# Contextual attention on one core: the additions of the shifted copies move from VectorE to GpSimd

## The reference

```
f = b[:, :, ::2, ::2]                       # 40 x 40
w = 3x3 patches of f                        # L = 1600 patches of 64*9
wn = w / max(|w|, 1e-4)
yi = einsum(w, wn) * mm                     # 1600 x 1600 scores
yi = softmax(10 * yi over the patches) * mm
patches = einsum(yi, 4x4 patches of b with stride 2)
out = the patches added up where they overlap (stride 2), cropped, / 4
```

## Time and profile before

| | |
|---|---|
| median of 3 runs | 1432.39 us |
| the profiled execution | 1435.39 us, its span 1433.6 us |
| TensorE busy | 1327.2 us (93%) |
| VectorE busy | 1183.3 us (83%) |
| ScalarE busy | 857.9 us (60%) |
| GpSimd busy | 46.9 us (3%) |
| line 979 on VectorE | 448 additions, 247.6 us |
| line 1109 on GpSimd | 56 copies, 42.9 us |

### The profile page before, as it was taken

The page is one execution under the profiler, slowest core; times in us unless marked ns, Lnnn a source line. Parts: engine busy times, 40 slices in busy tenths (PEclk is TensorE's granted clock), DMA queues, the critical chain, the costliest instruction groups (busy, mean ns, idle before and its releaser), DMA issues.

```text
span 1433.6 us, 24384 instructions
## 1 busy us (share of the span) xinstructions
PE 1327.2 (93%) x7190; PEld 894.6 (62%) x7190; DVE 1183.3 (83%) x2827; ACT 857.9 (60%) x2233; POOL 46.9 (3%) x62
## 2 busy tenths in 40 slices
PE   4988999999999899999999899999999999998886
PEld 4756765676556665577656676567655766566433
DVE  3667889799888898889897888979987898978983
ACT  2677646676557565586565764666655855658331
POOL 1000000010000100001000000001000010000100
PEclk9997999999999999999999999999999999999998
DMA  5502482145822556135741359224572236313442
GB/s 91 89 1 85 109 173 76 47 116 119 163 64 67 124 113 150 49 86 127 143 117 33 104 118 179 70 52 110 126 156 67 71 107 135 94 32 96 131 136 53
DMA packets 180471, 142.54 MB, mean 99 GB/s; under 512 B 119859, under 2 KB 177267, under 8 KB 180339
## 3 DMA queue, kind: packets, MB, share of 16 engines
q1 hardware_dynamic: 180178, 140.50, 41.7%
q10 hardware_dynamic: 160, 0.49, 0.2%
HBM read 19.76 MB, written 13.11 MB: 23 GB/s over the span
## 4 chain that ended last, share of the span: by engine, by line
PE 54%; DVE 15%; ACT 11%; issue 8%; SPq 7%; DMA 5%; DVEq 0%; POOL 0%; ACTq 0%; POOLq 0%
PE psO L521 26%; PE psG L471 23%; SPq L326 4%; DVE G L968 4%; ACT S L697 4%; DVE Z L1001 3%; DMA SH<-G 3%; PE psG L480 3%; DVE S L898 3%; ACT G L708 2%; ACT G L683 2%; DVE G L979 2%; DMA SHJ<-G 2%; SPq L270 1%; ACT SQ L624 1%
## 5 line engine op out<-in xcount | busy, mean ns | idle before, releaser
L521 PE MATMUL psO<-Z,B 123*128 123x492 f32 (+2 forms) x1792 | 718.6, 530 | 46.0 <-DVE Z L1001 31.4
L521 PEld LDWEIGHTS psO<-Z,B 123*128 123x128 f32 x1792 | 325.8, 194 | 247.6 <-issue 133.8
L471 PE MATMUL psG<-LH,HL 128*123 128x246 f16 (+2 forms) x2616 | 407.2, 285 | 3.7 <-ACT G L670 3.0
L697 ACT ACTIVATE S<-S,nm 123x480 f32<-123x480 f32 (+3 forms) x560 | 308.5, 555 | 161.2 <-DVE nm L905 160.8
L471 PEld LDWEIGHTS psG<-LH,HL 128*123 128x123 f16 x2616 | 277.4, 137 | 125.4 <-issue 64.5
L708 ACT ACTIVATE G<-G,nb 123x492 f32<-123x492 f32 (+1 forms) x448 | 265.0, 639 | 60.3 <-DVE G L968 59.9
L898 DVE CUSTOM_DVE_ANT_0 S<-G,RB 123x492 f32<-123x492 f32 (+1 forms) x448 | 268.4, 604 | 25.8 <-ACT G L683 15.6
L979 DVE TENSOR_TENSOR G<-G,SH 123x492 f32<-123x492 f32 (+1 forms) x448 | 247.6, 591 | 48.9 <-DMA SH<-G 48.3
L968 DVE SCALAR_TENSOR_TENSOR G<-G,RA,psB 123x492 f32<-123x492 f32 (+1 forms) x448 | 270.4, 647 | 0.0
L883 DVE TENSOR_TENSOR G<-G,psG 123x492 f32<-123x492 f32 (+2 forms) x272 | 135.0, 496 | 90.4 <-PE psG L471 46.5
L1001 DVE TENSOR_TENSOR Z<-G 123x984 f32<-123x984 f32 (+2 forms) x192 | 197.2, 1028 | 0.0
(11 more groups left out here) (79 smaller groups left out, 575.8 us busy)
## 6 DMA issues: line engine op xcount, KB each, us to landing
SH<-G SPq DMA_DIRECT2D x336, 214.8 KB
SH<-G SPq DMA_DIRECT2D x112, 89.2 KB
SH<-G SPq DMA_DIRECT2D x336, 19.2 KB
XP<-x SPq DMA_DIRECT2D x20, 280.0 KB, 5.7
XP<-mid SPq DMA_DIRECT2D x20, 280.0 KB, 5.5
HL<-LH SPq DMA_DIRECT2D x16, 246.5 KB, 4.5
mid<-OSB SPq DMA_DIRECT2D x48, 80.0 KB, 2.3
out<-OSB SPq DMA_DIRECT2D x48, 80.0 KB, 2.3
```

What stands on the lines that cost most here:

```text
L471: last = pe.matmul(psG[0:TW, bank, b0 * TW:b1 * TW], st[:, v % 2, p:p + TW], mv[:, v % 2, lo:lo + n], start=i == 0, stop=i == len(terms) - 1)
L521: last = pe.matmul(psO[:, b, 0:n], B[:, o:o + 128], Z[:, 2 * (s % 2) + j, 0:n], start=t == 0, stop=t == TILES - 1)
L697: last = act.activation(y, y, ACT.Exp, bias=nm[:, k * TILES + t:k * TILES + t + 1], accum_out=sg[:, c:c + 1])
```

## The change

GpSimd makes the additions of line 979 in place of VectorE. They stand first in GpSimd's slots, ahead of the wraps, and are those of pair s + 3 in slot s (AHEAD was 2). Order, tiles, operands, waits and counts of each addition are as before; no other engine's order is changed. The wraps stay in their slots.

```diff
-AHEAD = 2
+AHEAD = 3
...
-            def add_shifted(at):        # in VectorE's block
...
-                    at_y = place(u, v, s + AHEAD)
-                    if at_y:
-                        add_shifted(at_y)
                     at_z = place(u, v, s + 1)
                     if at_z:
                         sum_pair(at_z, s + 1)
...
+            def add_shifted(at):        # in GpSimd's block
+                u, k, i = at
+                c0, n = p_cols(k)
+                for j, t in enumerate(arg_tiles(i)):
+                    o = k * TILES + 2 * i + j
+                    pool.wait_ge(sh_in[o % SFREE], (u * (NB // SFREE) + o // SFREE + 1) * 16 * len(SHIFT_PARTS))
+                    g = G[:, t * GLEN + c0:t * GLEN + c0 + n]
+                    pool.tensor_tensor(g, g, SH[:, o % SFREE, 0:n], ALU.add).then_inc(y1_made, 1)
+
             def body(u, v):
                 for s in BODY:
+                    at = place(u, v, s + AHEAD)
+                    if at:
+                        add_shifted(at)
                     if s < 5 and u is not None:
                         wrap(u, s + 2)
```

More of the change, by code:

```diff
@@ L970, in argument_pair @@
                                              op0=ALU.mult, op1=ALU.subtract).then_inc(arg_made, 1)
-            def add_shifted(at):
[L973 to L979, removed]
             def sum_pair(at, s):
```

## The result

The change made the kernel slower. Eight runs after have a median of 1438.85 us (1436.86 to 1443.50), eight runs before 1430.06 us (1426.80 to 1433.05); the ratio is 1.0066, with a 95% interval of 1.0048 to 1.0085. The forecast was 1419 us, faster. The profiled execution after took 1443.5 us, the longest of its eight; the one before, 1435.39 us, is likewise longer than its eight.

What follows compares the result with a forecast made beforehand. TensorE and VectorE were taken as both full mid-image, with winnable time where TensorE waits for VectorE's Z. Borders 8, clock 3, last image 2, middles 0 us: -13 us, 1419 us for the median, own range 1409 to 1428 (chance 0.48).

Steps and rivals of the forecast that it cites:

- (4) Middles: 0: Middle of an image: TensorE is full and hides VectorE's relief, so the change gains 0 us there.
- 7 us, hidden: A pair's four DMAs (2.9 us), landing (2.0) and two additions (2.2) fit in the 12 us before the first sum.
- a gain for SP: SP's 236.8 us of waits for line 979 to free SH slots would shrink, as GpSimd frees them once data lands.
- Speed of GpSimd: A GpSimd addition of 492 columns takes 1.1 us, between 0.73 and 1.46, fast enough for slots of 6.1 us.
- Price of the lock, in the mean: VectorE's operations with two SBUF inputs (lines 898, 1001) wait for GpSimd's reads: 0.6 us a slot, between 0 and 2.2.
- Relief of VectorE: VectorE loses a pair's additions, 1.16 us a slot; net of the lock's price 0.56 us a slot.
- Term 1: Eight borders between images, where VectorE is full and TensorE waits for Z: 1.0 us gained at each, 8 us.
- the first rival: Nothing gained: GpSimd's additions fall on the border's last two of line 898; 1432 us, chance 0.16.
- Term 2: Around the borders, shorter TensorE idle time keeps its clock up at some: a quarter of 12 us, 3 us.
- Term 3: Last image, only shifts, sums and pastes, TensorE and VectorE both full: 2 us gained.
- A larger AHEAD only says where the additions stand before the wraps: GpSimd's own order: AHEAD of 3 has no cost, since GpSimd has no pace but its waits.
- The third: Slower if lock waits pass 1.16 us a slot, at lines 898 and 1001 around borders: 1444 us, chance 0.18.

Runs made afterwards that it cites:

- pieces and AHEAD = 3: Changed kernel with the loads as one DMA in each of slots 2 to 4 and 9 to 14: 1428.41 us, 0.9976 of the kernel before.
- small loads: Loads from the second unit on bring one row: changed kernel 1418.82 us, kernel before with the same loads 1425.30 us; ratio of the two 0.9966.
- memset_long: Changed kernel with each GpSimd addition replaced by writing zeros of about the same time, additions left out: 1406.74 us, 0.9823 of the kernel before.

## Why the prediction was wrong

The direction was wrong: 9 us slower, where 13 us faster was forecast. Of the 22 us between them, about 14 come with the traffic of the loads, a term that the sum did not have, and 8 are gains that were put too high.

**The step that failed** is "(4) Middles: 0", with the chain "7 us, hidden" and the mean price of the lock that it rests on. The chain of four issues, a landing and two additions was worked out for an undisturbed slot. Behind the loads of slots 3 and 9 a shift is ready for its addition 5.5 us after its last issue in place of 2.2, several pairs come at once, and GpSimd adds without a break. There VectorE's sum, maximum and negation each meet an addition: 2.5 us in slot 12 of image 3, where the forecast had 0.6 us a slot. VectorE can't set against it the 1.16 us of its own additions, since it spends the freed time waiting for the landing (40.8 us in 8 waits). The matmuls of the next scores wait for VectorE (13.9 us, from 0.2), and TensorE's clock falls behind some of these waits. In the table this is 0.0066 - (-0.0034) = 1.0%, 14 us. Some 6 us of them go when the loads come in pieces, and with them these waits (5.8 and 0.2 us). This much is shown for the jams, and with AHEAD = 3 alone: with 2 the waits are much the same, and bunching costs this change nothing beyond what it costs VectorE's kernel. The other 9 us go only with the bytes, and how they arise stays open.

The row that should have told of the jams stood in the waits of the kernel before, 120 to 1320 us, and was not read: VectorE's additions waited for the shifts 36.6 us in 17 times, up to 4.8 us, some two times an image. The landings were late already.

```profile
DVE G L979 <- DMA SH<-G: 36.6, 17, 4.8
```

The other row on this path, was read as a gain for SP, and that was right: SP waits 14.8 us for GpSimd's additions in place of 236.8. No run shows that it bought anything.

**Speed of GpSimd.** Right in size: the shortest addition of 492 columns took 1.21 us and started 1.19 us apart in a full queue, where 1.1 was taken and 1.46 was the bound. The estimate from the Trainium skill (GPSIMD Engine Reference, section 3.1) was 1.07 us plus dispatch; the trace agrees.

**Price of the lock, in the mean.** Nearly right: 0.68 us a slot against 0.6. But what it costs is not told by the mean, as above, and its list of meetings was too short. Line 905, 2 columns and one input, was not on it and took 32 of the 152 us. The Trainium skill (SBUF — State Buffer, "Who interferes with whom") names tensor_scalar and copy among the operations that can take the shared port pair; the trace agrees for this one, 311 ns against 169, and 262 beside a GpSimd that only writes. The page was cited for the two-input case alone.

**Relief of VectorE.** Somewhat too high: 72.9 us of busy time less is 0.33 us a slot; the forecast had 0.56, because it counted every pair as a long one (a quarter of them are short) and the lock a little low.

**Term 1, borders, 8 us.** Mis-sized. A mean price does not tell what a border pays: the price falls on the last maximum and the negation, which were the path, 1.91 us in the border shown against 1.16 removed. TensorE's wait for this Z fell from 18.9 to 17.0 us, not to 10. This is the first rival, additions that land just on the last of line 898, and its alignment was right to the operation; it had 0.16.

**Term 2, clock, 3 us**, depended on term 1 and did not come at the borders: 6 of the eight stretches of 15 us, moved by the delay, have a granted clock under 1.00, 0.77 in two as before. In images 1 and 3 the clock fell at the jams as well, which the forecast did not have.

**Term 3, last image, 2 us**, came in the profiled executions as a number, but not by its mechanism. From the last image's first sum to the end of the span after takes 114.0 us in place of 117.9. The sums themselves gain nothing (from the first to the last the two traces differ by 0.6 us or less). Three of the 3.9 us lie in the last 16 matmuls, 4.68 us at a granted clock of 1.00 in place of 7.73 at 0.60, behind a shorter wait. TensorE of the kernel before, then of after:

```profile
1419.40 7.73 PE L521 MATMUL psO<-Z,B 123*128 123x328 f32 x16 [4.59 <-DVE Z L1001]
```

```profile
1430.54 4.68 PE L521 MATMUL psO<-Z,B 123*128 123x328 f32 x16 [2.34 <-DVE Z L992]
```

It is a matter of luck too: with pieces and AHEAD = 3 these matmuls take 7.78 us. Over all runs, what is left of the forecast's 13 us is the 0.34% with small loads, 5 us.

**"A larger AHEAD only says where the additions stand before the wraps"**: wrong here. It costs 0.5% with the loads bunched. The profiled executions of the two kernels drift apart by up to 3 us an image, at the border and at both jams, and no single wait carries it; the granted clock would, by the estimate above. Why it stays up with AHEAD = 2 is not settled.

**The rivals.** The third, slower by the shared read, had the right sign and the right resource, and 1444 us was 5 us above the time. But its condition, that the waits of a slot pass 1.16 us, was not met in the mean (0.68), and it expected "hardly any in the middles", where most of the loss is. Without the lock there is no loss (memset_long, 0.9823), and without load traffic there is none (0.9966 of its counterpart): it takes both. That is shown for the totals. That a held-up VectorE can't catch up between jams is not shown: in the table it catches up in part, in most images.

## What to carry to other kernels

Moving work from VectorE to GpSimd is priced at the operations that are on the path where it lands, not by the mean over a slot: list every operation of VectorE's that GpSimd's reads hold up, the small ones too, and lay the transfers' landings beside them in the trace. Check the slack behind the worst landing, where the moved work comes in one burst, and not in the typical slot. A long wait that a moved operation ends need not be its fault: see when the data landed, and compare with the wait before the change. When large loads share a queue with copies that others wait for, issuing them in single pieces can be worth more than moving the work: here 0.5%, with the additions left where they were.

## What the runs showed of the hardware that was not expected

- A VectorE tensor_scalar of 2 columns, 0.17 us alone, took up to 1.16 us beside a GpSimd addition, and 0.26 us in the mean beside GpSimd's writes of zeros (1.17 us each); with zeros of 0.55 us its mean was 0.18. Maxima and sums did not move beside these writes.
- A GpSimd copy of 1230 columns (1.38 us in the mean, with its own waits) held up VectorE as an addition of 492 columns did (1.42): 778 and 783 ns for the maxima, 1444 and 1442 for the sums. What counted here is that GpSimd reads SBUF for this long, not what it computes.
- Taking most bytes of the loads away gave VectorE's kernel no more than sending them in pieces did: 1425.30 and 1425.05 us.
